# Causal head attention run head by head, with the mask summed in PSUM and the row sums divided out after the value product

## What is computed

```python
def pattention(x, K, V):
    a = softmax(EMB ** -0.5 * einsum('btc,nc->btn', x, K), axis=-1)   # 512 parameter rows
    return einsum('btn,nc->btc', a, V)

def causal_sdpa(q, k, v):                                             # 16 heads of 32 columns
    scores = einsum('bhqd,bhkd->bhqk', q, k) / sqrt(32)
    scores = where(tril(ones((T, T))), scores, -inf)
    return einsum('bhqk,bhkd->bhqd', softmax(scores, axis=-1), v)

k = pattention(h, kK, kV); q = pattention(h, qK, qV); v = pattention(h, vK, vV)
o = causal_sdpa(to_heads(q), to_heads(k), to_heads(v))
o = pattention(o, pK, pV)
x = o + x_in
x = pattention(layer_norm(x), fK, fV) + x                             # 2048 parameter rows
```

## Time and profile before

| | |
|---|---|
| median of three executions | 568.1 us (568.1 to 571.04) |
| the profiled execution | 569.73 us, its span 567.8 us |
| granted PE clock over the span | 0.949 |
| PE busy | 501.1 us (88%) |
| DVE busy | 435.3 us (77%) |
| ACT busy | 333.7 us (59%) |
| POOL busy | 26.7 us (5%) |
| the heads and the p pattention | 280.25 to 327.70 us of the span |

### The profile page before, as it was taken

The page is one execution under the profiler, slowest core; times in us unless marked ns, Lnnn a source line. Parts: engine busy times, 40 slices in busy tenths (PEclk is TensorE's granted clock), DMA queues, the critical chain, the costliest instruction groups (busy, mean ns, idle before and its releaser), DMA issues.

```text
span 567.8 us, 10906 instructions
## 1 busy us (share of the span) xinstructions
PE 501.1 (88%) x4131; PEld 337.7 (59%) x4131; DVE 435.3 (77%) x695; ACT 333.7 (59%) x645; POOL 26.7 (5%) x97
## 2 busy tenths in 40 slices
PE   5989999999999697499946879894899999999995
PEld 1444544445444254279834758673778888888873
DVE  2378777787778776858787576898888998998984
ACT  2544554445553345446477536984587887888772
POOL 3000000000003200000000000001000000000000
PEclk9999999999999797889957999996899999999999
DMA  8899888888887200506500220378678987986001
GB/s 337 307 354 382 333 336 326 321 329 328 324 325 278 75 1 2 200 23 226 197 22 2 74 75 0 149 279 312 222 275 319 347 309 280 384 314 215 0 1 40
DMA packets 35936, 122.44 MB, mean 216 GB/s; under 512 B 2609, under 2 KB 2609, under 8 KB 31282
## 3 DMA queue, kind: packets, MB, share of 16 engines
q1 hardware_dynamic: 35602, 121.27, 56.5%
q10 hardware_dynamic: 288, 0.52, 0.3%
HBM read 121.26 MB, written 0.52 MB: 214 GB/s over the span
## 4 chain that ended last, share of the span: by engine, by line
PE 43%; DVE 11%; ACT 6%; issue 1%; DVEq 0%; ACTq 0%
PE score_banks L910 15%; PE bank L943 8%; PE score_banks L626 3%; PE score_banks L672 2%; PE score_banks L870 2%; PE score_banks L767 2%; PE score_banks L791 1%; DVE w_split L1649 1%; ACT arena L1163 1%; DVE arena L1575 1%; PE bank L767 1%; PE bank L919 1%; PE bank L505 1%; PE bank L626 1%; PE bank L636 1%
## 5 line engine op out<-in xcount | busy, mean ns | idle before, releaser
L991 ACT ACTIVATE xprobs<-score_banks,small 128x512 f32<-128x512 f32 (+1 forms) x104 | 67.9, 664 | 104.8 <-DVEq L1395 69.3
L1520 DVE TENSOR_TENSOR w_split<-arena,w_split 128x1024 fp32r<-128x1024 f32 x96 | 114.3, 1221 | 6.6 <-ACT w_split L1118 4.4
L1118 ACT ACTIVATE w_split<-arena 128x1024 fp32r<-128x1024 f32 x96 | 100.8, 1060 | 14.8 <-PE score_banks L910 10.5
L459 PE MATMUL bank<-arena,wi_sb 128*64 128x512 f32 (+1 forms) x400 | 93.5, 609 | 6.3 <-DMA arena<-in_ctxT 6.3
L910 PE MATMUL score_banks<-w_split,xg 128*128 128x512 f32 x384 | 88.7, 390 | 1.4 <-ACT xg L1283 1.4
L1404 DVE STREAM_TRANSPOSE xprobsT<-xprobs 128x1024 f32<-128x1024 f32 (+1 forms) x52 | 61.6, 1184 | 34.9 <-ACT xprobs L991 33.6
L910 PEld LDWEIGHTS score_banks<-w_split,xg 128*128 128x128 f32 x384 | 71.8, 188 | 17.1 <-ACT xg L1283 1.7
L1376 DVE TENSOR_REDUCE small<-score_banks 128x2 f32<-128x1024 f32 (+1 forms) x52 | 57.4, 1139 | 16.0 <-PE score_banks L490 16.0
L459 PEld LDWEIGHTS bank<-arena,wi_sb 128*64 128x64 f32 x400 | 27.0, 140 | 56.1 <-issue 54.6
L490 PE MATMUL score_banks<-k_full,hT 64*32 64x256 f32 (+1 forms) x1664 | 51.7, 382 | 9.4 <-ACT xprobs L991 8.2
L505 PE MATMUL bank<-xprobsT,v_rows 128*64 128x256 f32 x392 | 48.6, 391 | 0.0
(11 more groups left out here) (263 smaller groups left out, 709.0 us busy)
## 6 DMA issues: line engine op xcount, KB each, us to landing
arena<-in_ctxT SPq DMA_DIRECT2D x23, 2048.0 KB, 8.7
arena<-in_w12T SPq DMA_DIRECT2D x32, 1024.0 KB, 5.9
arena<-in_w3T SPq DMA_DIRECT2D x16, 1024.0 KB, 5.5
arena<-in_fKT SPq DMA_DIRECT2D x4, 1024.0 KB, 7.3
arena<-in_fV SPq DMA_DIRECT2D x4, 1024.0 KB, 5.1
arena<-in_ctxT SPq DMA_DIRECT2D x4, 512.0 KB, 6.2
arena<-in_Wo SPq DMA_DIRECT2D x1, 2048.0 KB, 13.0
arena<-in_kKT SPq DMA_DIRECT2D x1, 1024.0 KB, 10.7
```

What stands on the lines that cost most here:

```text
L459: last = pe.matmul(kp_bank[b][DH * h:DH * (h + 1), 0:half], wi_sb[:, k, :], ctx_buf[:, b, k, h * half:(h + 1) * half], start=(k == 0), sto ...
L991: act.activation(xprobs[:, qb, 0:2 * width].rearrange("p (h n) -> p h n", h=2), score_banks[:, 2 * p:2 * p + 2, 256 * q:256 * q + width], ...
L1118: act.activation(w_split[:, i % 4, 0, :], raw, ACT.Copy).then_inc(part_high, 1)
L1520: return dve.tensor_tensor(w_split[:, i % 4, 1, :], raw, w_split[:, i % 4, 0, :].bitcast(F32), ALU.subtract)
```

## The change

What the change does, engine by engine:

- **PE** first multiplies an identity (`ident_r`) with the mask (`mask_r`) into a head's bank (`head_mask`, 384 columns, fp32r) and then adds the scores to it (`head_scores`, `start=False`). Banks come from a ring of five, `HEAD_BANKS`. The order is written by pairs of heads: masks and scores of pair w+2, then the transposes of pair w. Between them stand, once for a chunk, `turn_rsum` and `head_out`. The v pattention's second product is cut up, with the scores of heads 0 to 3 between its parts. `p_scores(k)`, a quarter of the p pattention's first product for both token tiles, takes the place of `key_scores("p", ...)`; three of the four quarters stand before the end of the heads.
- **DVE** takes the row maxima from PSUM, head by head, with the sign turned in the same instruction (`head_max`), copies the transposed blocks of the odd heads (`head_odd_out`), and multiplies a chunk's value product with the reciprocal sums (`scale_heads`). Adding the mask and normalizing the probabilities are gone.
- **ACT** takes the exponentials from PSUM (`head_exp`) and copies the transposed blocks of the even heads (`head_even_out`). The factor HSCALE is applied to `qh` once. The split of pV comes behind the heads, in two halves.
- **The row sums** go from DVE (`head_rsum`) to POOL, which writes each of them 32 times (`spread_rsum`), to PE, which transposes them (`turn_rsum`) into the free half of the output bank, and to DVE, which copies them to `hT` (`take_rsum`).
- **POOL** also makes the low half of pK (two instructions of 128x1024, before on DVE) and splits the result of chunks 0 to 2 (`split_heads`).
- Two ACT copies that make `ident_r` and `mask_r` stand ahead of ACT's second superstep of the cross-attention.

The diff, without the code that it takes out (it stands above) and without small changes of banks and semaphore counts:

```diff
+        ident_r = sb("ident_r", [P, P], F32R)
+        mask_r = sb("mask_r", [P, 3 * P], F32R)
...
-        hp = ctx_flat[:, 0:3072].rearrange("p (b r k) -> p b r k", b=2, r=HPC)
+        hp = ctx_flat[:, 2048:5120].rearrange("p (b r k) -> p b r k", b=2, r=HPC)
         hp0, hp1 = hp[:, :, :, 0:P], hp[:, :, :, P:3 * P]
-        hpT = ctx_flat[:, 4096:7168].rearrange("p (b r k) -> p b r k", b=2, r=HPC)
+        hpT = ctx_flat[:, 5120:8192].rearrange("p (b r k) -> p b r k", b=2, r=HPC)
+        rsum_rows = probsT[:].rearrange("p g n -> p (g n)")[:, 1024:1280].rearrange("p (s r d) -> p s r d", s=ST, r=HPC)
+        HEAD_BANKS = [score_banks[:, i, :] for i in range(4)] + [bank[0]]
+        head_out_bank = bank[1]
...
+            for g, ring, raw in halves("pK"):
+                pool.wait_ge(ev("attn_high"), g + 1)
+                pool.tensor_tensor(w_split[:, ring, 1, :], raw, w_split[:, ring, 0, :].bitcast(F32),
+                                   ALU.subtract).then_inc(ev("pK_low"), 1)
+            def spread_rsum(c):
+                pool.wait_ge(ev("head_rsum"), c + 1)
+                if c:
+                    pool.wait_ge(ev("head_out"), c)
+                pool.tensor_copy(rsum_rows, h_rsum[:, c].unsqueeze(3).broadcast_to([P, ST, HPC, D])).then_inc(ev("rsum_spread"), 1)
+            def split_heads(c):
+                pool.wait_ge(ev("heads_scaled"), c + 1)
+                pool.tensor_copy(hT_split[0][:, c, :], hT[:, c, :]).then_inc(ev("o_high"), 1)
+                pool.wait_ge(ev("o_high"), c + 1)
+                pool.tensor_tensor(hT_split[1][:, c, :], hT[:, c, :], hT_split[0][:, c, :].bitcast(F32),
+                                   ALU.subtract).then_inc(ev("o_low"), 1)
+            spread_rsum(0)
+            for c in range(KC - 1):
+                spread_rsum(c + 1)
+                split_heads(c)
...
+            def rows_out(m, st, bk, rows=range(NT)):
...
+            def head_mask(i):
+                if i < 2:
+                    pe.wait_ge(ev("kh_done"), 2)
+                    pe.wait_ge(ev("mask_ready"), 2)
+                elif i < 4:
+                    pe.wait_ge(ev("qh_done"), 2)
+                elif i == 4:
+                    pe.wait_ge(ev("vh_done"), 1)
+                else:
+                    pe.wait_ge(ev("head_probs"), 2 * (i - 5) + 2)
+                pe.matmul(HEAD_BANKS[i % 5][:, 0:3 * P], ident_r[:], mask_r[:], start=True, stop=False)
+            def head_scores(i):
+                bk, c, rows = HEAD_BANKS[i % 5], i // HPC, slice(D * (i % HPC), D * (i % HPC + 1))
+                pe.matmul(bk[:, 0:P], qh[rows, c, 0:P], kh[rows, c, 0:P], start=False, stop=False)
+                pe.matmul(bk[:, P:3 * P], qh[rows, c, P:T], kh[rows, c, :], start=False, stop=True).then_inc(ev("head_scores"), 1)
+            def head_pair(w):
+                for i in (2 * w, 2 * w + 1):
+                    head_mask(i)
+                pe.wait_ge(ev("qh_done"), 2)
+                for i in (2 * w, 2 * w + 1):
+                    head_scores(i)
...
+            def head_turn(i):
+                pe.wait_ge(ev("head_probs"), 2 * i + 2)
+                if i >= 2:
+                    pe.wait_ge(ev("head_even_out" if i % 2 == 0 else "head_odd_out"), i // 2)
...
+            def turn_rsum(c):
...
+                else:
+                    pe.wait_ge(ev("heads_scaled"), c)
+                pe.wait_ge(ev("rsum_spread"), c + 1)
+                for st in range(ST):
+                    last = pe.transpose(head_out_bank[:, T + st * P:T + (st + 1) * P], rsum_rows[:, st].rearrange("p r d -> p (r d)"), ident[:])
+                last.then_inc(ev("rsum_turned"), 1)
             def head_out(c):
...
+                pe.wait_ge(ev("rsum_taken"), c + 1)
+                pe.wait_ge(ev("head_even_out"), 2 * c + 2)
+                pe.wait_ge(ev("head_odd_out"), 2 * c + 2)
...
+            def p_scores(k):
+                if k == 0:
+                    split_ready("pK")
+                    pe.wait_ge(ev("head_probs"), 2 * 12 + 2)
+                if k < KC - 1:
+                    pe.wait_ge(ev("o_low"), k + 1)
+                else:
+                    pe.wait_ge(ev("hT_done"), ST * TURNS.index("oT") + 2)
+                w = split_tile("pK", k)
+                for st in range(ST):
+                    for a, (x, y) in enumerate(THREE):
+                        last = pe.matmul(B[1 + st], hT_split[x][:, k, st * P:(st + 1) * P], w[y], start=(k == 0 and a == 0),
+                                         stop=(k == KC - 1 and a == 2))
+                    if k == KC - 1:
+                        last.then_inc(ev("key_scores"), 1)
...
+            head_mask(0)
+            head_mask(1)
+            rows_out("v", 0, B[4], (0, 1))
+            pe.wait_ge(ev("qh_done"), 2)
+            head_scores(0)
+            head_scores(1)
+            rows_out("v", 0, B[4], (2, 3))
+            head_pair(1)
+            rows_out("v", 1, B[5])
+            for w in range(6):
+                if w in (2, 4):
+                    turn_rsum(w // 2 - 1)
+                head_pair(w + 2)
+                if w in (2, 4):
+                    head_out(w // 2 - 1)
+                head_turn(2 * w)
+                head_turn(2 * w + 1)
+            turn_rsum(2)
+            head_turn(12)
             head_out(2)
+            head_turn(13)
+            p_scores(0)
+            head_turn(14)
+            head_turn(15)
+            p_scores(1)
+            turn_rsum(3)
+            p_scores(2)
             head_out(3)
...
+            p_scores(3)
...
+            act.wait_ge(ident_done, 1)
+            act.activation(ident_r[:], ident[:], ACT.Copy).then_inc(ev("mask_ready"), 1)
+            act.wait_ge(causal_done, 2)
+            act.activation(mask_r[:], causal[:].rearrange("p b k -> p (b k)"), ACT.Copy).then_inc(ev("mask_ready"), 1)
...
+            def head_even_out(i):
+                act.wait_ge(ev("head_turned"), i + 1)
+                if i >= 2 * HPC:
+                    act.wait_ge(ev("head_out"), i // HPC - 1)
+                act.activation(hpT[:, (i // HPC) % 2, i % HPC, :], T6[:, 0:3 * P], ACT.Copy).then_inc(ev("head_even_out"), 1)
+            def head_exp(i):
+                bk, c, r = HEAD_BANKS[i % 5], i // HPC, i % HPC
+                if i >= 2 * HPC:
+                    act.wait_ge(ev("head_turned"), i - 2 * HPC + 1)
+                act.wait_ge(ev("head_bias"), 2 * i + 2)
+                for half, (part, cols) in enumerate(((hp0, slice(0, P)), (hp1, slice(P, 3 * P)))):
+                    act.activation(part[:, c % 2, r, :], bk[:, cols], ACT.Exp, bias=h_bias[:, c, half, r:r + 1],
+                                   accum_out=h_sum[:, c, half, r:r + 1]).then_inc(ev("head_probs"), 1)
+            head_exp(0)
+            head_exp(1)
+            for w in range(1, 8):
+                head_exp(2 * w)
+                head_even_out(2 * w - 2)
+                head_exp(2 * w + 1)
+            head_even_out(14)
+            attn_high("pV", 0, 1)
+            act.wait_ge(ev("heads_scaled"), KC)
+            act.activation(hT_split[0][:, KC - 1, :], hT[:, KC - 1, :], ACT.Copy).then_inc(ev("hT_high"), 2)
+            attn_high("pV", 1, 2)
...
+            dve.tensor_scalar(qh[:, 2:4, :].rearrange("p c t -> p (c t)"), B[3], HSCALE, None, ALU.mult).then_inc(ev("qh_done"), 1)
+            def head_max(i):
+                dve.wait_ge(ev("head_scores"), i + 1)
+                bk, c, r = HEAD_BANKS[i % 5], i // HPC, i % HPC
+                for half, cols in enumerate((slice(0, P), slice(P, 3 * P))):
+                    dve.tensor_reduce(h_bias[:, c, half, r:r + 1], bk[:, cols], AX.X, ALU.max, negate=True).then_inc(ev("head_bias"), 1)
+            def head_odd_out(i):
+                dve.wait_ge(ev("head_turned"), i + 1)
+                if i >= 2 * HPC:
+                    dve.wait_ge(ev("head_out"), i // HPC - 1)
+                dve.tensor_copy(hpT[:, (i // HPC) % 2, i % HPC, :], T7[:, 0:3 * P]).then_inc(ev("head_odd_out"), 1)
+            def head_rsum(c):
+                dve.wait_ge(ev("head_probs"), 2 * HPC * (c + 1))
+                dve.reciprocal(h_rsum[:, c], h_sum[:, c]).then_inc(ev("head_rsum"), 1)
+            def take_rsum(c):
+                dve.wait_ge(ev("rsum_turned"), c + 1)
+                dve.tensor_copy(hT[:, c, :], head_out_bank[:, T:2 * T]).then_inc(ev("rsum_taken"), 1)
+            def scale_heads(c):
+                dve.wait_ge(ev("rsum_taken"), c + 1)
+                dve.wait_ge(ev("head_out"), c + 1)
+                dve.tensor_tensor(hT[:, c, :], head_out_bank[:, 0:T], hT[:, c, :], ALU.mult).then_inc(ev("heads_scaled"), 1)
...
+                if st == 0:
+                    head_max(3)
+            for w in range(8):
+                if w in (2, 4, 6):
+                    take_rsum(w // 2 - 1)
+                if w < 6:
+                    head_max(2 * w + 4)
+                    head_max(2 * w + 5)
+                if w in (2, 4, 6):
+                    scale_heads(w // 2 - 1)
```

(12 more changed lines are left out.)

140 lines of the change are left out of this document (26 added, 114 removed).

## The result

The changed kernel takes **564.8 us** (median of five executions, 563.5 to 565.7), beside 568.1 us for the kernel before. The ratio is 0.9935, with a 95% interval of 0.991 to 0.9959: 0.65% faster, by an amount that can be told from no change. The forecast was 563.4 us. The profiled execution took 565.72 us, its span 563.9; PE was busy 505.0 us (before 501.1), DVE 425.0 (435.3), ACT 328.4 (333.7), POOL 36.3 (26.7), and the granted clock over the span was 0.962 (0.949).

What follows compares the result with a forecast made beforehand. It took the stage to be bound by chunk order and a slow PE. A full-clock gain of 8.3 us, less 3.0 for one low stretch and 0.6 for handoffs and POOL, gave 4.7: 563.4 us from 568.1, range 558.0 to 568.6.

Steps and rivals of the forecast that it cites:

- the signs that I named: Right: p pattention ends near 323, three POOL waits about 1.2 us, chunks 5.5 to 6 us, stage clock 0.85 to 0.95.
- What bounded the kernel: Heads to p pattention, 47.45 us: no engine full; bound by chunk hand-round order and a PE slow at its turn.
- Masks, maxima, POOL's spread, the wait: Per chunk: mask 0.18 us each, maxima 0.27 and 0.41, POOL's row-sum spread 0.42, PE's added wait 1.2.
- A chunk's period: Four heads: PE's 4.5 us of work plus 1.2 wait, 5.7 us, over ACT's 4.6 and DVE's 4.7.
- The sum at full clock: From the v product at 274.69, the p pattention's end at 319.4 instead of 327.7 us: 8.3 us gained.
- The clock: In the stage, one fall to half clock likely, costing 3.0 us; the forecast with it had chance 0.37.
- The rival that the clock stays up: No low stretch in the stage: gain 8.3, 559.8 us, or 557.5 with faster scores; chance 0.24.
- The rule on bank cycling: Skill's rule: the ring of five PSUM banks would not stay at full clock; second rival, 566.4 us, chance 0.22.
- The slower rival: PE at 1.2 GHz all through the stage: 15.8 us lost against 8.3 gained, 575.6 us; chance 0.08.
- The round trip binds: A head's trip through ACT, PE and copies exceeds a pair's 2.85 us, adding 4.4 in all: 567.2 us; chance 0.09.
- Moves at no cost: pK's low half on POOL (2 x 2.35 us) hidden; two ACT copies in the cross-attention, under 0.9 us, taken as 0.
- What followed: The f pattention and experts, behind the p pattention, depend on its end and are moved as they are.

Runs made afterwards that it cites:

- e7: Kernel before, without the eight multiplications that normalize the heads' probabilities (reciprocals stay): 568.2 us, ratio 0.9996 to the kernel before.
- e3: Kernel before, with 32 unused filling matmuls where PE waits for the heads' softmax: 569.6 us, ratio 1.0014 to the kernel before.
- e2: Changed kernel with 27 unused filling matmuls where PE waits behind the heads: 562.9 us, ratio 0.989 to the kernel before.
- e11: Changed kernel with the mask added by DVE in PSUM instead of by PE matmuls: 572.6 us, ratio 1.0095 to the kernel before.
- e12: Mask added by DVE in the changed kernel, plus ten filling matmuls in each of PE's first three row-sum waits: 569.1 us, ratio 1.0003 to the kernel before.
- e6: Changed kernel with one more unread 128x128 copy on ACT for each head, 16 in all: 565.1 us, ratio 0.9928 to the kernel before.
- e10: Changed kernel with the low half of pK back on DVE, ahead of the first maximum: 564.5 us, ratio 0.9936 to the kernel before.
- e4: Changed kernel with the first three quarters of the p scores moved behind the last value product: 563.9 us, ratio 0.9912 to the kernel before.
- e1: Changed kernel with row sums' transposes behind the next pair's scores and value product behind that pair's transposes: 561.9 us, ratio 0.9901 to the kernel before.
- e9: Changed kernel with row sums' transposes moved later, also for the last chunk but one, and DVE's copy between two maxima: 561.4 us, ratio 0.9887 to before.

## Why the prediction was right, step by step

The time (563.4 forecast, 564.8 measured) and the end of the p pattention (323.0 by the forecast's sum, 323.04 measured) agree. The gain by the ratio is 3.7 us against 4.7. That the end agrees so well is luck, two errors that cancelled in the stage: at full clock it is 2.0 us longer than my sum, of which I had allowed 0.6, and it lost 1.6 us to the clock and not 3.0. Of the signs that I named, two lie outside what I had called right without reaching what I had called wrong: chunks 6.32 us apart (5.5 to 6; wrong over 6.5) and a clock of 0.96 in the stage (0.85 to 0.95). The low stretches are one in the stage and a second behind it.

- **What bounded the kernel.** The order in which chunks go round, and a slow PE: right, as far as these runs tell, and the two can't be taken apart as a sum. Of the stage of the kernel before, leaving out the normalization takes 0.3 us (e7) and taking out half of the low clock 0.7 (e3); the change took 4.9. No run has the old order with the clock up all through.
- **Masks, maxima, POOL's spread, the wait.** Forecast 0.18, 0.27 and 0.41, 0.42, 1.2 three times; measured 0.175, 0.29 and 0.42, 0.40, 1.09 three times. Right.
- **A chunk's period.** Forecast 5.7, measured 6.32 with the clock at 1.00. The step "so a chunk takes 4.5 + 1.2" was mis-sized. PE's list by the chain is 5.23: row sums 0.41, masks and scores 2 x 1.21, value product 0.79, transposes 2 x 0.81. Against my 4.5: the scores of a pair took 0.86, not 0.75, so 0.22 (the bound of 0.92 was near the truth, since a pair costs almost what four heads do); the first transpose behind a matmul of another shape took 0.26, not 0.11, twice, so 0.30; the row sums' transposes 0.41, not 0.22, so 0.19; the value product 0.03. These parts are from end to end, as the chain has them. From start to start PE's list is the same 5.23 (row sums 0.17, masks and scores 2 x 1.38, value product 0.79, transposes 0.63 and 0.88), so how the excess of 0.7 divides depends on the count, and its sum does not. The wait was 0.11 shorter. Twice 0.6 is 1.2 us of the 8.3 forecast at full clock.
- **The sum at full clock.** Heads 4 to 7 start at 282.89 (282.5), the first row sums at 288.17 (287.2), the last but one at 300.80 (298.6), the last value product ends at 308.9 (the tail's 7.8 us was 8.1), `p_scores(3)` starts at 310.53 (308.0). From there to the end 12.5 us, less the 1.6 of the low stretch 10.9, against 11.4. So at full clock the stage would have ended near 321.4, a gain of 6.3 and not of 8.3.
- **The clock.** "One low stretch, 3.0", among the heads. Wrong in place: among the heads the clock was 1.00, in the whole stage 0.96. It fell behind them, twice for 3.4 us; e2 prices these at 1.6 and 1.1 us. That the sum, 2.7, is near my 3.0 is luck. The rival that the clock stays up is therefore the one that held for the heads; its time was missed because the terms were short by 2 us.
- **The rule on bank cycling.** The ring of five banks ran at a clock of 1.00 with an idle of 1.09 us in each 6.32; with idles of 2.3 us (e11) it fell. e12, which has the same ring, fillers and shorter idles, held the clock too in its profiled execution. The section of the Trainium skill that I weighed ("TensorE: Matmul & The Clock Gate", "A second HAM failure mode: psum-queue depth-cycling") tells of a kernel that cycles through banks and goes back and forth between the two clocks. The heads of e11 did so, those of the change did not.
- **The slower rival.** "PE at 1.2 GHz all through", 9.9 us a chunk, 575.6 us. It did not come, but a kernel near to it exists: e11, with 20.5 us of low clock among the heads, has chunks of 9.5 and 9.8 us and 572.6 us. It differs from the change in where the mask is added. On PE that costs 0.35 us a pair and 0.7 a chunk; on DVE it costs the stage 7.7 us more.
- **The round trip binds.** No: ACT took 16 more copies with no effect (e6).
- **Moves at no cost.** pK's low half on POOL: right, and no gain either (e10). The early p scores, which I counted in the tail: no loss without them (e4). The two ACT copies in the cross-attention: taken as 0, and no run tells, since the first row of the table varies by 3 us.
- **What followed.** I took the f pattention as moved, as it is. It took 1.2 us more, for the second low stretch.

Open: what makes a low stretch come in one execution and not in another of the same program, so that the profile of e1 has none in the stage or the f pattention and that of e9, with less idle time, has one; and what sets the length of the one in front of the experts, 13.6, 17.1 or 20.5 us. The experts took 165.3 to 165.7 us behind the first length and 167.0 to 168.6 behind the others.

## What to carry to other kernels

When the trace names one step as the releaser of a long wait, ask what comes just behind it: here 7 us of DVE's work could be left out for 0.3 us of the stage and none of the time, since the other engine's queue was as late. Work added to a nearly full PE can pay, if it takes a slower engine's step out of a round trip for which PE waits: the price is on PE's list, the gain is a shorter wait and the clock that goes with it. Then look at where the wait stands in the queue: with the row sums behind the next pair's scores instead of ahead of them, and DVE's copy in time for it, the same instructions took 1 us less a chunk (e9). And look at the clock of all executions before a difference between two profiles is put down to an edit.

## What the runs showed of the hardware

- A stretch of low clock can last 3.41 us; those in the trace of before were 6.8 to 13.7, others here 17.1 and 20.5. One began with the p pattention's second product and had PE busy in all of its 3.4 us; ahead of it PE had waited 1.66, 1.09 and 1.36 us, with 1.7 and 0.7 us of work between.
- The rounds of heads held a granted clock of 1.00 with a wait of 1.09 us in each. With the mask on DVE, waits of 2.3 us (and one of 0.84), they fell to 0.50; with the same mask and fillers in the waits, the profiled execution was back at 1.00.
- Executions of one program differ in their low clock: twelve of e12 had 36 to 49 us of it, worked out from clock and span.
- Two heads' scores, in 32 rows each, took 0.86 us, four heads' 0.92; a transpose of 128 columns takes 0.11 us in a row and, from end to end, 0.26 as the first behind scores or a value product.
- POOL copied 128x256 with a broadcast input in 0.40 us, and subtracted 128x1024 in 2.38.
